# Feed-forward and shared expert on 628 in place of 640 token columns, and an expert's results copied out at the start of the next second unit

## What is computed

```python
# graph layer, behind the attention: h1 is 625 x 512, W1 512 x 2048, W2 2048 x 512
h2 = layer_norm(h1, ln2_g, ln2_b)
h2 = gelu(h2 @ W1 + b1) @ W2 + b2
x = x + h1 + h2
# mixture: 8 experts of 512 x 1024, two for a token, and one shared expert for all
xt = _layernorm(x)
shared = silu(xt @ sw1) * (xt @ sw3) @ sw2
h = silu(einsum('td,edh->eth', xt, w1)) * einsum('td,edh->eth', xt, w3)
y = einsum('eth,ehd->etd', h, w2)
out = einsum('te,etd->td', comb, y) + shared      # comb: the two gates of a token
x = x + out
```

## Time and profile before

| | us |
|---|---|
| median of three runs | 856.68 |
| the profiled execution | 855.59 |
| its span, first to last instruction | 854.0 |
| attention and all before it | to about 333 |
| feed-forward | 344 to 456 |
| shared expert with routing | 458 to 548 |
| routed experts | 548 to about 825 |
| gather of results, rest of the shared expert, output | to 854 |

### The profile page before, as it was taken

How to read it: one execution, slowest core, us unless ns; L and a number is a source line. 1 busy time by engine, 2 the same in 40 slices (tenths; PEclk the granted TensorE clock), 3 DMA queues, 4 the chain that set the end, 5 groups by cost and what they waited for, 6 DMA issues and landing times. The chain is left out here.

```text
span 854.0 us, 13328 instructions
## 1 busy us (share of the span) xinstructions
PE 767.4 (90%) x4993; PEld 640.5 (75%) x4993; DVE 554.9 (65%) x904; ACT 460.8 (54%) x748; POOL 301.0 (35%) x189
## 2 busy tenths in 40 slices
PE   3997799999999978899996999799889899898894
PEld 2664588787878753899995999688788787786784
DVE  6628997979797926454226444478686786777755
ACT  4244596868686825633334332356565665566530
POOL 8240686868686820000000004033222222232333
PEclk9999799999999989899998699999999999999998
DMA  9320830000000006000004208756565766556015
GB/s 260 119 41 9 298 67 2 1 2 2 1 2 2 1 9 251 1 1 1 2 0 152 71 1 297 249 175 224 174 237 193 231 207 210 194 196 218 34 37 162
DMA packets 66460, 92.46 MB, mean 108 GB/s; under 512 B 6723, under 2 KB 44197, under 8 KB 65877
## 3 DMA queue, kind: packets, MB, share of 16 engines
q1 hardware_dynamic: 64149, 85.77, 30.9%
q0 software_dynamic: 2240, 5.76, 2.2%
HBM read 80.69 MB, written 10.82 MB: 107 GB/s over the span
## 5 line engine op out<-in xcount | busy, mean ns | idle before, releaser
L1581 POOL TENSOR_TENSOR w_lo<-weights_far,w_hi 128x1024 fp32r<-128x1024 f32 x32 | 77.0, 2406 | 210.9 <-ACT w_hi L1699 210.9
L660 POOL TENSOR_TENSOR bias_exp_hi<-edge_exp_hi,mask 128x640 fp32r<-128x640 f32 x40 | 98.0, 2451 | 71.3 <-PE ps L806 32.3
L1784 PE MATMUL ps<-xT,w_hi 128*128 128x480 f32 (+7 forms) x512 | 112.1, 342 | 3.6 <-DVE w_lo L1601 3.6
L1784 PEld LDWEIGHTS ps<-xT,w_hi 128*128 128x128 f32 x512 | 84.6, 194 | 9.9 <-issue 4.1
L1786 PEld LDWEIGHTS ps<-xT,w_lo 128*128 128x128 f32 x512 | 74.7, 192 | 1.7
L1786 PE MATMUL ps<-xT,w_lo 128*128 128x240 f32 (+7 forms) x512 | 75.4, 270 | 0.0
L806 PE MATMUL ps<-onehot,bias_exp_hi 128*128 128x314 f32 x400 | 69.5, 320 | 5.4 <-POOL bias_exp_hi L660 5.0
L1799 PE MATMUL ps<-w_hi,hidden_hi 128*128 128x512 f32 (+7 forms) x120 | 52.1, 434 | 23.0 <-DVE weights_near L1629 21.0
L1618 DVE TENSOR_TENSOR hT<-hT 128x240 f32<-128x240 f32 (+7 forms) x64 | 63.2, 988 | 11.3 <-ACT hT L1716 11.3
L1699 ACT ACTIVATE w_hi<-weights_far 128x1024 fp32r<-128x1024 f32 x64 | 67.1, 1050 | 0.0
L806 PE MATMUL ps<-onehot,bias_exp_lo 128*128 128x314 f32 x400 | 65.7, 311 | 0.0
(11 more groups left out here) (272 smaller groups left out, 1678.8 us busy)
## 6 DMA issues: line engine op xcount, KB each, us to landing
weights_far<-in_L_ffn_w SPq DMA_DIRECT2D x64, 512.0 KB, 5.5
weights_near<-in_L_ffn_w SPq DMA_DIRECT2D x32, 512.0 KB, 3.6
weights_near<-in_L_gnn_W SPq DMA_DIRECT2D x1, 4096.0 KB, 14.5
weights_near<-in_L_gnn_Wqkv SPq DMA_DIRECT2D x3, 1024.0 KB, 8.2
weights_ff<-in_L_gnn_W SPq DMA_DIRECT2D x1, 3072.0 KB, 13.9
weights_lo_shared<-in_L_ffn_sw SPq DMA_DIRECT2D x6, 512.0 KB, 7.7
weights_near<-in_L_ffn_sw SPq DMA_DIRECT2D x6, 512.0 KB, 6.7
slot_rows<-zeros SPq DMA_DIRECT2D x1, 2944.0 KB, 26.1
```

The lines of the kernel that those rows point to most:

```text
L660: pool.tensor_tensor(to.rearrange("p t (h d) -> p t h d", h=H), e[:, b, :, :].unsqueeze(3).broadcast_to([P, CT, H, BN]), m.unsqueeze(2).br ...
L1581: pool.tensor_tensor(w2s[u][1], raw_rest[2] if v == V else raw[u][2], w2s[u][0], ALU.subtract)\
L1784: pe.matmul(both(bank, cap), w[u % 2][0][:, c, cut], xT(r)[:, c, :, :], start=c == 0, stop=False)
```

## The change

In feed-forward and shared expert the tensors of hidden features have 628 columns for 640, the halves 314 for 320, and the last token tile of `down` 116 rows for 128 (`OWN`). In the routed experts `results(r - 1)` stands at another place of VectorE's list. The core of the diff (the same replacements of HALF by SH and of NP by SRC in ScalarE's and VectorE's operations, in the tensors' shapes and in the rest of the shared expert are left out):

```diff
+OWN = SRC - (NT - 1) * P
+def own_cut(t):
+    return slice(t * P, min((t + 1) * P, SRC))
+def own_rows(t):
+    return P if t < NT - 1 else OWN
...
             for t in range(NT):
+                n = own_rows(t)
                 dve.wait_ge(y_ps, t + 1)
-                dve.tensor_tensor(xs[:, t, :], xs[:, t, :], psum[t][:, :], ALU.add).then_inc(y_sb, 1)
+                dve.tensor_tensor(xs[0:n, t, :], xs[0:n, t, :], psum[t][0:n, :], ALU.add).then_inc(y_sb, 1)
...
-                        last = pe.matmul(psum[t][:, :], hid[m % 2][hp][:, t * P:(t + 1) * P], w2s[m % 4][wp],
+                        last = pe.matmul(psum[t][0:own_rows(t), :], hid[m % 2][hp][:, own_cut(t)], w2s[m % 4][wp],
...
-                            last = pe.matmul(up_bank[k % 3][:, 0:HALF], w1s[m % 2][wp][:, c, :],
-                                             rows_T[xp][:, c, half * HALF:(half + 1) * HALF], start=i == 0 and c == 0,
+                            last = pe.matmul(up_bank[k % 3][:, 0:SH], w1s[m % 2][wp][:, c, :],
+                                             rows_T[xp][:, c, half * SH:(half + 1) * SH], start=i == 0 and c == 0,
...
                 weights_lo(v + 1, 0)
+                if u == 1 and r:
+                    results(r - 1)
                 parts_summed(v, 0)
                 weights_lo(v + 1, 1)
                 hidden(v, 0)
-                if u == 1 and r:
-                    results(r - 1)
                 parts_summed(v, 1)
```

More of the change, by code:

```diff
@@ L867, in feed_forward @@
         w2s = [[sb(f"ff_w2_{part}{i}", [P, D]) for part in parts] for i in range(4)]
-        hid = [[sb(f"ff_hidden_{part}{i}", [P, NP]) for part in parts] for i in range(2)]
-        h32 = [sb(f"ff_hidden{i}", [P, NP], F32) for i in range(2)]
+        hid = [[sb(f"ff_hidden_{part}{i}", [P, SRC]) for part in parts] for i in range(2)]
+        h32 = [sb(f"ff_hidden{i}", [P, SRC], F32) for i in range(2)]
         feed_forward_units(nc, sem, finished, x, W2, rows_b, rows_c, wo, w_near, w_far, xs, hT, vs, work, small, ident, psum,
@@ L1087, in routing @@
         w2s = [[sb(f"sh_w2_{part}{i}", [P, D]) for part in parts] for i in range(4)]
-        hid = [[sb(f"sh_hidden_{part}{i}", [P, NP]) for part in parts] for i in range(2)]
-        h32 = [sb(f"sh_hidden{i}", [P, NP], F32) for i in range(2)]
-        gated = [sb(f"sh_gated{i}", [P, HALF], F32) for i in range(2)]
+        hid = [[sb(f"sh_hidden_{part}{i}", [P, SRC]) for part in parts] for i in range(2)]
+        h32 = [sb(f"sh_hidden{i}", [P, SRC], F32) for i in range(2)]
+        gated = [sb(f"sh_gated{i}", [P, SH], F32) for i in range(2)]
         routing_units(nc, sem, w_in, gate_w, biases, w1, w3, w2, sw1, sw3, sw2, rows_d, slots, xs, hT, vs, work,
@@ L1374, in up @@
                             for c in range(DC):
-                                last = pe.matmul(up_bank[k % 3][:, 0:HALF], split(n, m)[wp][:, c, :],
-                                                 rows_T[xp][:, c, half * HALF:(half + 1) * HALF],
+                                last = pe.matmul(up_bank[k % 3][:, 0:SH], split(n, m)[wp][:, c, :],
+                                                 rows_T[xp][:, c, half * SH:(half + 1) * SH],
                                                  start=i == 0 and c == 0, stop=i == 2 and c == DC - 1)
@@ L1397, in down @@
                     for i, (hp, wp) in enumerate(passes):
-                        last = pe.matmul(psum[t][:, :], hid[m % 2][hp][:, t * P:(t + 1) * P], split(2, m)[wp],
+                        last = pe.matmul(psum[t][0:own_rows(t), :], hid[m % 2][hp][:, own_cut(t)], split(2, m)[wp],
                                          start=m == 0 and i == 0, stop=m == HS - 1 and i == 2)
@@ L1490, in routed_units @@
     h32_all, rest = free[:, 0:UM * NP], free[:, UM * NP:]
-    gated = [rest[:, i * HALF:(i + 1) * HALF] for i in range(2)]
+    h32_own = free[:, 0:UM * SRC]
+    gated = [rest[:, i * SH:(i + 1) * SH] for i in range(2)]
     y_st = [slots[0][:, SLOT - (CB - i) * D:SLOT - (CB - 1 - i) * D] for i in range(CB)]
-    hid_rest = [[hid_all[i][:, 0:NP], xT_all[0][:, i * NP:(i + 1) * NP]] for i in range(2)]
-    h32_rest = h32_all.rearrange("p (m n) -> p m n", m=UM)
+    hid_rest = [[hid_all[i][:, 0:SRC], xT_all[0][:, i * SRC:(i + 1) * SRC]] for i in range(2)]
+    h32_rest = h32_own.rearrange("p (m n) -> p m n", m=UM)
     names = gate_views(gate_sb)
@@ L1813, in rest_up @@
                         for c in range(DC):
-                            last = pe.matmul(rest_bank[i % 3][:, 0:HALF], w[0][wp][:, c, m * P:(m + 1) * P],
-                                             rows_T[xp][:, c, half * HALF:(half + 1) * HALF],
+                            last = pe.matmul(rest_bank[i % 3][:, 0:SH], w[0][wp][:, c, m * P:(m + 1) * P],
+                                             rows_T[xp][:, c, half * SH:(half + 1) * SH],
                                              start=j == 0 and c == 0, stop=j == 2 and c == DC - 1)
@@ L1825, in rest_down @@
                     for i, (hp, wp) in enumerate(passes):
-                        last = pe.matmul(rest_out[t], hid_rest[hp][m][:, t * P:(t + 1) * P], w2s[0][wp][:, m, :],
+                        last = pe.matmul(rest_out[t][0:own_rows(t), :], hid_rest[hp][m][:, own_cut(t)], w2s[0][wp][:, m, :],
                                          start=m == 0 and i == 0, stop=m == UM - 1 and i == 2)
```

17 lines of the change are left out of this document (9 added, 8 removed).

## The result

| | before | after |
|---|---|---|
| median, runs taken together on one chip | 856.89 us (854.65 to 857.95) | 844.64 us (841.28 to 845.64) |
| ratio | | 0.9854, 95% interval 0.982 to 0.9887 |
| profiled execution, its span | 855.59, 854.0 | 845.64, 844.0 |
| feed-forward, first start of `up` to the start of the last matmul of `down` | 112.38 | 112.39 |
| GpSimd's starts, from one ahead of the first results unit to the last (27 intervals) | 224.75 | 212.19 |

The kernel is 12.3 us faster, against a forecast of 841.0, some 15 us. The last line of the table is the ruler for the rest of this text: in before it runs from a start at 595.47, one ahead of the first of the earlier trace rows, to the one at 820.22, in after from 596.34 to 808.53.

What follows compares the result with a forecast made beforehand. TensorE bounds feed-forward and shared expert; in the routed experts a GpSimd, VectorE, ScalarE ring sets the beat, held by TensorE's waits for result copies. 13.1 + 1.9 = 15.0 us off 855.59 gives 840.6, stated as 841.0; range 835.5 to 847.5.

Steps and rivals of the forecast that it cites:

- The ring: Routed experts: GpSimd, VectorE, ScalarE and GpSimd again release each other in turn; 7.51 us in a unit without results.
- the interval behind a results unit: Routed experts: time between GpSimd starts after a unit that copies results, held by TensorE's late `up`; seven sum to 71.0 us.
- Part 1: Routed experts: moving the copies in front of `parts_summed` gains 18.6 + 3.5 - 8.9 = 13.1 us.
- The price of the copies: Routed experts: the moved copies delay `parts_summed` and GpSimd's next start by 1.27 us, seven times, 8.9 us; bounds 0 to 1.27 each.
- The seven intervals behind: GpSimd's intervals after results units fall to their neighbours' length, 71.0 to 52.4 us, a gain of 18.6.
- the six after those: The next GpSimd intervals, where TensorE still catches up, fall from 48.8 to 45.3 us, gaining 3.5; bounds 0 and 3.5.
- The wait for the copies in the unit with 176 columns: TensorE's wait before `down` in that routed-expert unit falls from 2.79 to 0.97 us.
- TensorE stays the bound: Rival, chance 0.12: slow stretches remain or appear elsewhere and TensorE doesn't get ahead in the routed experts; 846 us.
- The copies cost nothing: Rival, chance 0.07: ScalarE and VectorE absorb the 1.27 us of each moved pair; 831.7 us.
- the ring pays and isn't shortened: Rival, chance 0.03: TensorE doesn't hold the interval behind results, so the copies only add seven times 1.27; 862.6 us.
- Part 2: Feed-forward and shared expert: 628 columns save 672 x 2.5 ns, 1.7 us, plus 0.2 at the lower clock; 1.9, bounds 0 and 2.
- the catching-up intervals: GpSimd's intervals one after those behind results units; if they stay, the forecast's own range ends at 844.5 us.

Runs made afterwards that it cites:

- part 1 alone: The kernel before with only the two result copies moved in front of `parts_summed`, 640 columns kept: 845.02 us, ratio 0.9802 to before.
- one copy late: The changed kernel with only the first bank's copy at the new place, the second's back behind `hidden(v, 0)`: 843.54 us, ratio 0.9794 to before.
- the version that moves them there: The changed kernel with both copies under GpSimd's operation in unit u = 0, halves of 320 and 308, hidden tiles 640 wide: 831.88 us, 0.9703 of before.
- copies covered: The changed kernel with both copies moved to unit u = 0, between `parts_summed(v, 1)` and `hidden(v, 1)`: 835.85 us, ratio 0.9707 to before.
- extra copy covered: The kernel with both copies under GpSimd's operation, plus one unread 512-column copy ahead of each two: 837.57 us, one run.
- the open extra copy: The changed kernel plus one unread 512-column copy ahead of each two, at their place behind the first weight part: 851.19 us, one run.
- the second execution of the same kernel: The changed kernel, unaltered, run once more beside before on the chip of the first follow-up runs: 843.53 us, ratio 0.9798.

## Why the prediction was right where it was, and where it wasn't

**What bounds the kernel** was read rightly. The ring GpSimd, VectorE, ScalarE set the pace, and the interval behind a results unit was TensorE's.

**Part 1, 13.1 us forecast, 12.6 measured on the ruler** (13.1 in part 1 alone; the 0.6 between them is after's one stretch at the lower level). The price of the copies was forecast as 7 times 1.27 = 8.9; it is 8.4. The pair of copies lasts 1.27, but the piece that it pushes back grows by 1.2 only. The seven intervals behind gained 18.1 (forecast 18.6), the six after those 2.8 (forecast 3.5). The wait for the copies in the unit with 176 columns was forecast at 0.97 and is 1.48, since `up` now ends 0.65 us before the copies start and not 0.14 (argued: TensorE has lost nothing to the lower clock before it); the seven sum to 11.2 for some 13. The prediction drew on the Trainium skill, SBUF — State Buffer, section Who interferes with whom; the traces agree with that rule, and by more than one row now: three copies beside GpSimd's operation cost nothing (203.20 against 203.27 us on the ruler), while every copy in front of `parts_summed` costs 0.6.

**TensorE stays the bound** (0.12) was wrong for after but for the 0.6 us in its fifth expert, where a wait of 1.94 us was followed by the lower level as this rival had it, and right one step away from it: with one copy late, TensorE holds the ring for two intervals of each of the first four experts and one of the fifth. The prediction had put its room at 0.8 us for four units of the widest expert, and that was about right; I didn't take that number to my own experiment, where I expected 4.2 us and got none.

**The copies cost nothing** and **the ring pays and isn't shortened** have fallen with the two tables of intervals. Copies that cost nothing do exist, at another place: the version that moves them there comes out at 831.88, near this rival's 831.7 us.

**Part 2, 1.9 us forecast.** This is the step that failed, by its size. The term was 672 matmuls times 2.5 ns, and the slope holds: `up` is 2.3 ns shorter. What failed is the sentence that `down` costs nothing because its moving operand keeps 512 columns: it is 3.1 ns longer in each of 240 matmuls, 0.74 us in feed-forward alone, against 0.88 us that 384 shorter `up` save. What is left by the period is 7 ns in each of 16 chunks, 0.1 us, and feed-forward as a whole shows none of it (112.38 and 112.39). An estimate from the same two differences for the six chunks of the shared expert (288 `up`, 90 `down`) is 0.66 less 0.28, some 0.4 us more; their stretch took 73.8 to 77.0 us in executions of kernels with the same code there, so no run can show it. That is 0.5 of the 1.9 us forecast. Which bytes of a stationary operand make a matmul slower is not settled. Shown is that in feed-forward the 116-wide tile costs 20 ns a chunk, the even halves another 20, and the tiles 628 wide 6.

**The sum.** 15.0 was forecast, 12.6 came from the ruler and nothing that can be seen from the columns; the medians differ by 12.3. For the profiled execution the forecast was 840.6 and 845.64 was measured: the 5.0 us between them are the 1.9 of the columns, 0.5 on the ruler, 0.9 by which the stretch is entered later and 1.7 behind the last start. The range (835.5 to 847.5) held by its margins for a rival and for the clock; 844.64 is just outside the forecast's own 836 to 844.5, and not for the reason that its upper bound stood for, since the catching-up intervals did shorten.

## What to carry over

Ask of each instruction on a shared engine what its neighbour would be doing meanwhile: work put under a wait that exists anyway is free as far as it fits (1.9 us did here), and the place that frees another engine earliest (part 1) can be worth 8 us less than the covered one beside it. A place that serves one engine halfway can make that engine the bound, so count its room before splitting. Cutting a matmul's operand to the rows in use saves only moving columns; a narrower or shifted stationary tile should be timed from start to start, since it can take all of it back.

## What the runs showed of the hardware

- In feed-forward, matmuls with 512 moving columns settle at 227 ns from start to start with stationary tiles of 128 columns, and stand at 233 with one of 116. With tiles of hidden features that are 628 wide, and the narrow last tile, the mean is 231.5 for 228.4, and chunks take 6918 and 6948 ns in turn; 640 wide, every chunk takes the same. In the routed experts tiles of 16 to 112 columns make no difference by width (229.8 to 231.7).
- 12 moving columns less are 7 ns (147 to 140), where the slope of the prediction gives 5.
- A VectorE product of two SBUF operands that starts beside GpSimd's operation ends 0.15 to 0.33 us after it, in all 31 cases of each of five traces (before, after, one copy late, copies covered, extra copy covered): it lasts 2.11, 1.42 or 0.85 us, as it starts later. Three copies from PSUM in the same place last their usual 0.68 (one) and 1.28 us (two).
- TensorE's clock fell to the 1.2 GHz level at five places between 565.7 us and the last results in before, at two in after, and at none with one copy late (waits for copies of at most 2.1 us) or with the copies covered (its longest other wait in the loop 1.7 us). The length of the wait doesn't decide: in the kernel with the open extra copy one of 1.69 us was followed by the lower level and one of 2.05 wasn't, and the wait of 1.94 us in the fifth expert was followed by it in after and not in the second execution of the same kernel. So I give no rule.
